# A fused attention and feed-forward kernel on one core: one program instead of two, the norm chain in items, eight probability slots and one split slot, with a new plan

## What is computed

```python
xn = layernorm(x)                                   # over the 256 features, eps 1e-5
q = einsum('bld,dhk->blhk', xn, Wq)                 # 16 heads of 64
latent = einsum('bld,dc->blc', xn, Wkv_down)        # 64 wide
k = einsum('blc,chk->blhk', latent, Wk_up)
v = einsum('blc,chk->blhk', latent, Wv_up)
attn = softmax(causal(einsum('bqhd,bkhd->bhqk', q, k) / 8))
y = einsum('bhqk,bkhd->bqhd', attn, v)
out = x + einsum('bqhd,hdo->bqo', y, Wout) + tanh(xn @ weight @ aux1 @ aux2 + bias)
```

## Time and profile before

| | us |
|---|---|
| median of 3 executions | 2101.32 (2099.3 to 2105.44) |
| the profiled execution | 2102.5 |
| its span in the trace | 2100.8 |
| PE busy | 2008.7 (96%) |
| DVE busy | 1651.9 (79%) |
| POOL busy | 1352.5 (64%) |
| ACT busy | 1108.7 (53%) |

### The profile page before, as it was taken

The page is one execution under the profiler, slowest core; times in us unless marked ns, Lnnn a source line. Parts: engine busy times, 40 slices in busy tenths (PEclk is TensorE's granted clock), DMA queues, the critical chain, the costliest instruction groups (busy, mean ns, idle before and its releaser), DMA issues.

```text
span 2100.8 us, 35430 instructions
## 1 busy us (share of the span) xinstructions
PE 2008.7 (96%) x11192; PEld 1329.4 (63%) x11192; DVE 1651.9 (79%) x3875; ACT 1108.7 (53%) x2075; POOL 1352.5 (64%) x1163
## 2 busy tenths in 40 slices
PE   7999999989999899999999999999999999999996
PEld 6666666656666566666666666666666666666563
DVE  4778778788778888778878878788878788778773
ACT  3455555545555455554555555555455555555553
POOL 0466666765666657676667756666567656667766
PEclk7999999999999999999999999999999999999998
DMA  3112111111111201121111211112111121111110
GB/s 99 32 34 60 37 41 42 37 54 35 47 37 42 59 24 42 47 62 37 45 34 37 67 37 37 39 40 62 37 37 37 44 59 37 42 37 34 52 36 25
DMA packets 83396, 91.37 MB, mean 43 GB/s; under 512 B 12304, under 2 KB 66448, under 8 KB 83216
## 3 DMA queue, kind: packets, MB, share of 16 engines
q1 hardware_dynamic: 83216, 89.11, 15.2%
HBM read 45.55 MB, written 8.91 MB: 26 GB/s over the span
## 4 chain that ended last, share of the span: by engine, by line
PE 71%; DVE 18%; issue 3%; DMA 2%; ACT 1%; SPq 1%; POOL 1%; POOLq 0%; ACTq 0%; DVEq 0%
PE ps L953 20%; PE ps L891 17%; PE ps L967 11%; PE ps L937 9%; PE ps L940 9%; DVE ps L1189 4%; PE ps L993 3%; DVE split_lo L1216 3%; DVE maxima L1194 2%; DVE rows L1205 1%; DVE xn L1281 1%; DVE y L1211 1%; DMA norm<-recips 1%; DVE stats L1251 1%; DVE maxima L1189 1%
## 5 line engine op out<-in xcount | busy, mean ns | idle before, releaser
L1335 POOL TENSOR_TENSOR p_sum<-p_sum,probs 128x512 f32<-128x512 f32 x672 | 899.8, 1366 | 264.1 <-ACT probs L1101 262.1
L1101 ACT ACTIVATE probs<-ps 128x512 f32<-128x512 f32 x1152 | 673.0, 597 | 461.3 <-PE ps L940 444.1
L1189 DVE CUSTOM_DVE_ANT_0 ps<-ps,causal 128x512 f32<-128x512 f32 (+3 forms) x1024 | 495.0, 502 | 160.3 <-PE ps L967 152.0
L953 PE MATMUL ps<-probs,latent 128*64 128x512 f32 x2304 | 525.7, 600 | 5.4 <-DVE q_lo L1305 5.4
L967 PE MATMUL ps<-k_hilo,q_hi 128*128 128x512 f32 (+3 forms) x1536 | 478.8, 362 | 22.4 <-DVE maxima L1189 14.1
L937 PE MATMUL ps<-q_hi,k_hilo 128*128 128x512 f32 x1152 | 479.6, 416 | 11.0 <-ACT probs L1101 9.9
L940 PE MATMUL ps<-q_lo,k_ones 65*128 65x512 f32 x1152 | 459.6, 399 | 0.0
L1335 POOL TENSOR_TENSOR p_sum<-probs 128x512 f32<-128x512 f32 x224 | 288.4, 1300 | 238.7 <-ACT probs L1101 237.5
L1194 DVE TENSOR_REDUCE maxima<-ps 128x1 f32<-128x512 f32 x512 | 352.0, 687 | 91.3 <-PE ps L967 88.1
L967 PEld LDWEIGHTS ps<-k_hilo,q_hi 128*128 128x128 f32 x1536 | 275.8, 191 | 130.4 <-issue 81.6
L953 PEld LDWEIGHTS ps<-probs,latent 128*64 128x64 f32 x2304 | 153.7, 137 | 306.8 <-issue 278.9
(11 more groups left out here) (101 smaller groups left out, 2326.1 us busy)
## 6 DMA issues: line engine op xcount, KB each, us to landing
q_hi<-q_hi SPq DMA_DIRECT2D x256, 128.0 KB, 2.4
norm<-recips SPq DMA_DIRECT2D x256, 128.0 KB, 2.9
x_in<-in_L_attn_x_bld SPq DMA_DIRECT2D x8, 1024.0 KB, 5.6
out_x<-acc SPq DMA_DIRECT2D x64, 128.0 KB, 1.7
q_lo<-rows SPq DMA_DIRECT2D x128, 4.0 KB
rows<-norm SPq DMA_DIRECT2D x128, 4.0 KB
recips<-rows SPq DMA_DIRECT2D x128, 4.0 KB
probs<-in_L_attn_Wq SPq DMA_DIRECT2D x1, 1024.0 KB, 7.7
```

The source lines that it names most:

```text
L953: last = nc.tensor.matmul(y_bank[g * LATENT:(g + 1) * LATENT, :], latent[par][:, key_block(unit, s), :], probs[:, t % PT_SLOTS, g * BANK:( ...
L1101: nc.scalar.activation(probs[:, t % PT_SLOTS, g * BANK:(g + 1) * BANK], ps[:, bank_of[kind, key], :], ACT.Exp).then_inc(exp_done, 1)
L1189: nc.vector.tensor_tensor_reduce(bank, bank, causal[:, BANK - w:BANK], 1.0, LOWEST, ALU.add, ALU.max, maxima[:, unit % 4, h, 0:1]).then_in ...
L1335: nc.gpsimd.tensor_tensor(sums, other, probs[:, slot, part], ALU.add).then_inc(pool_done, 1)
```

## The change

1. **One program.** `run` is called once with the two plans joined, so the barrier between them is gone, and engines pass from one plan to the other on their own. `bank_left` knows the last fold in a bank (kind `W`).
2. **First stage.** `x` of batch 0 comes by two DMAs with a semaphore each (later batches too), then Wq, Wk, and Wkv after those. `WARM` = 8 matmuls on the zeros of `causal` go ahead of the first transposes. The constants are made first on DVE, the fold of `wqk` stands around the second pair of transposes, `KN` after the queries, the remaining folds ahead of and between the eight maxima, and the subtractions for the low parts of `wvo` and `wff` after all maxima (`split wvo`).
3. **Repeated waits.** `wait_new` leaves out a wait of PE for a value that PE already waited for. On PE's matmuls 4,160 semaphores are named in place of 6,676.
4. **Norm chain in items.** LN1 is 13 items of one operation (the first: eight aggregations), planned 700 ns apart, each still followed by its own wait.
5. **Slots.** `SPLIT_SLOTS` 2 to 1, `PT_SLOTS` 7 to 8.
6. **The plan.** Other assumed costs and landings, extra time (`LATER`) before an item's input counts as ready, `SOON` 60 to 0, `LEAD` 13 to 11, feed-forward and the load of x earlier in a batch. PE goes 138 times to PVs and back instead of 133; the numbers of matmuls stay the same but for the 8 warm ones.

The diff, cut to its core:

```diff
-PT_SLOTS, Y_SLOTS, SPLIT_SLOTS, SUM_SLOTS, Q_BUFS = 7, 3, 2, 2, 3
+PT_SLOTS, Y_SLOTS, SPLIT_SLOTS, SUM_SLOTS, Q_BUFS = 8, 3, 1, 2, 3
-PE_TIME = {"ST": (462, 665), "PV": (846, 1070), "R": (462, 680), "MT": (60, 330), "O0": (693, 900),
+PE_TIME = {"ST": (462, 665), "PV": (859, 1080), "R": (462, 680), "MT": (60, 330), "O0": (715, 920),
...
-            "LN0": (800, 900), "LN1": (3000, 3200), "LN4": (1300, 1500)}
-LANDING = {"Q": 2900, "MT": 2300, "X": 6000, "RG": 2600, "RO": 2200, "RB": 4300}
+            "LN0": (800, 900), "LN1": (250, 350), "LN4": (1300, 1500)}
+LANDING = {"Q": 3500, "MT": 2300, "X": 7000, "RG": 3200, "RO": 2200, "RB": 4600}
+LATER = {"O": 2000, "R": 800, "MT": 800, "Q": 300}
-SOON = 60
-LEAD = 13
+SOON = 0
+LEAD = 11
-        self.f = [(b * STEPS + 3.5 * n + 1, (b, HALF_BLOCKS[n // 2][n % 2])) for b in range(batches)
+        self.f = [(b * STEPS + 3 * n + 1, (b, HALF_BLOCKS[n // 2][n % 2])) for b in range(batches)
-        self.x_at = [(b * STEPS + STEPS // 2 - 6, b + 1) for b in range(batches - 1)]
+        self.x_at = [(b * STEPS + STEPS // 2 - 12, b + 1) for b in range(batches - 1)]
...
                 if key[1] == 3:
-                    self.after(end, "LN1", key[0])
+                    for n in range(LN1_PARTS):
+                        self.after(end + 700 * n, "LN1", (key[0], n))
...
-                out.append((max(self.normal[u], bank), at, self.place_o))
+                out.append((max(self.normal[u] + LATER["O"], bank), at, self.place_o))
...
-            if late and (not st or step - late[1] > 1.5 or not idle_act):
+            if late and (not st or step - late[1] > 1.0 or not idle_act):
...
+    plan = [("W", "warm"), ("W", "constants")]
+    plan += [("LN0", (0, k)) for k in range(4)] + [("LN1", (0, n)) for n in range(LN1_PARTS)]
+    plan += [("LN4", (0, k)) for k in range(2)] + [("W", "turn wq"), ("W", "turn wk")]
+    plan += [("T", (0, c, 0)) for c in range(2)] + [("LN4", (0, k)) for k in range(2, 4)]
+    plan += [("TL", (0, c, 0)) for c in range(2)] + [("W", "casts"), ("W", "fold wqk 0")]
+    plan += [("T", (0, c, 1)) for c in range(2)] + [("TL", (0, c, 1)) for c in range(2)]
+    plan += [("W", "fold wqk 1")]
+    for side in range(2):
+        plan += [*two_parts("K", (0, side)), ("KL", (0, side))]
+    plan += [*two_parts("Q", (0, 0)), ("QL", (0, 0)), *two_parts("Q", (0, 1)), ("KN", 0)]
...
+            if what == "warm":
+                pe.wait_ge(consts_made, 1)
+                for n in range(WARM):
+                    nc.tensor.matmul(ps[:, 0, 0:BANK - P], causal[:, 0:P], causal[:, 0:BANK - P],
+                                     start=True, stop=True)
...
+            def wait_new(signal, value):
+                if reached.get(signal.num, 0) < value:
+                    reached[signal.num] = value
+                    pe.wait_ge(signal, value)
...
-        run(*first_plan(), load_all, make_constants)
-        run(*body_plan(B))
+        first, first_banks = first_plan()
+        body, body_banks = body_plan(B)
+        run(first + body, {**first_banks, **body_banks}, load_all, make_constants)
```

More of the change, by code:

```diff
@@ L195, in flush @@
                 if key[1] == 3:
-                    self.after(end, "LN1", key[0])
+                    for n in range(LN1_PARTS):
+                        self.after(end + 700 * n, "LN1", (key[0], n))
             elif kind == "LN1":
                 end = self.run("DVE", when, DVE_TIME[kind])
-                for k in range(2):
-                    self.after(end + 1000 * k, "LN4", (key, k))
+                if key[1] == LN1_PARTS - 1:
+                    for k in range(2):
+                        self.after(end + 1000 * k, "LN4", (key[0], k))
             elif kind == "LN4":
@@ L233, in choices @@
                 if q is not None:
-                    out.append((max(q, self.earliest("MAX")), self.max_at[self.n_max], self.place_max))
+                    out.append((max(q + LATER["Q"], self.earliest("MAX")), self.max_at[self.n_max], self.place_max))
         if "P1" in self.open:
@@ L239, in choices @@
             if self.turns:
-                out.append((max(self.max_end[self.turns[0]], bank), now - 9, self.place_mt))
+                out.append((max(self.max_end[self.turns[0]] + LATER["MT"], bank), now - 9, self.place_mt))
             if self.outs and self.block_added(self.outs[0][1]):
                 at, u = self.outs[0]
-                out.append((max(self.normal[u], bank), at, self.place_o))
+                out.append((max(self.normal[u] + LATER["O"], bank), at, self.place_o))
             if self.n_f < len(self.f) and (self.n_f < 2 or self.f[self.n_f - 2][1] in self.added):
@@ L292, in place_st @@
         if g == 1 and s == block_of(u):
-            self.sums.append((self.masked[-1], u))
+            self.sums.append((self.masked[-1] + LATER["R"], u))
     def place_max(self, ready):
@@ L489, in first_plan @@
 def first_plan():
[L492 to L502 removed]
+    plan = [("W", "warm"), ("W", "constants")]
[8 more added lines that the diff above has]
+    plan += [*two_parts("Q", (0, 0)), ("QL", (0, 0)), *two_parts("Q", (0, 1)), ("KN", 0)]
     maxima = [("MAX", c) for u in range(AHEAD) for c in max_chunks(u)]
[L504 to L506 removed]
+    plan += [("W", "turn others"), ("W", "fold aux"), *maxima[:2], ("QL", (0, 1)), maxima[2]]
+    plan += [("W", "fold wvo"), *maxima[3:6], ("W", "fold wff"), *maxima[6:]]
+    plan += [("MT", 0), ("W", "split wvo")]
     bank, n_p0, n_max = {}, 0, 0
@@ L515, in first_plan @@
         elif kind == "MT":
-            bank[kind, key] = 7
+            bank[kind, key] = 4
     return plan, bank
@@ L625, in build @@
         w_split = sem("w_split")
-        x_loaded = sem("x_loaded")
+        x_loaded = [sem(f"x_loaded{i}") for i in range(2)]
         ln_chain = sem("ln_chain")
@@ L864, in fold_on_dve @@
                         op1=ALU.subtract).then_inc(w_split, 1)
-            elif what == "fold wvo":
-                for n, bank in enumerate((5, 7, 6)):
-                    dve.wait_ge(w_copied, 14 + n)
+            elif what == "split wvo":
+                dve.wait_ge(w_copied, 17)
+                nc.vector.tensor_tensor(wff_lo[:, :, :].rearrange("p c n -> p (c n)"), ps[:, 0, :],
+                                        wff_hi[:, :, :].rearrange("p c n -> p (c n)").bitcast(F32),
+                                        ALU.subtract).then_inc(w_split, 1)
+                dve.wait_ge(w_copied, 18)
+                for n, bank in ((3, 1), (0, 5), (1, 7), (2, 6)):
                     nc.vector.tensor_tensor(wvo_part(wvo_lo, n), ps[:, bank, :],
@@ L1019, in tensor_program @@
                     b, c, half = key
-                    pe.wait_ge(xn_ready, 4 * count.of("LN1", b) + 2 * half + 2)
+                    wait_new(xn_ready, 4 * b + 2 * half + 2)
                     for k in range(4):
@@ new lines, in vector_program @@
+                    last = bits[:, 1, :].bitcast(F32) if n < 7 else guess
+                    if n == 0:
+                        for i in range(BLOCKS):
+                            done = nc.vector.bn_aggr(mean_var[:, i, :], stats[:, i, :])
+                    elif n == 1:
+                        done = nc.vector.tensor_scalar(var, mean_var[:, :, 1], EPS, None, ALU.add)
+                    elif n == 2:
+                        done = nc.vector.tensor_scalar(bits[:, 0, :], var.bitcast(I32), 1, None,
+                                                       ALU.logical_shift_right)
+                    elif n == 3:
+                        done = nc.vector.tensor_scalar(bits[:, 1, :], bits[:, 0, :], -1.0,
+                                                       RSQRT_BITS, ALU.mult, ALU.add)
+                    elif n % 3 == 1:
+                        done = nc.vector.tensor_tensor(square, last, last, ALU.mult)
+                    elif n % 3 == 2:
+                        done = nc.vector.scalar_tensor_tensor(
@@ L1274, in vector_program @@
+                    chained(done)
                 elif kind == "LN4":
@@ L1382, in sync_program @@
                     sp.wait_ge(ff_added, BLOCKS * key)
-                    sp.dma_start(x_in[:, :, :], x[key].rearrange("(i p) d -> p i d", p=P)
-                                 ).then_inc(x_loaded, 16)
+                    for half in range(2):
+                        sp.dma_start(x_in[:, 4 * half:4 * half + 4, :], x_rows(key, half)
+                                     ).then_inc(x_loaded[half], 16)
             for i in range(Q_BUFS):
```

176 lines of the change are left out of this document (75 added, 101 removed).

## The result

The changed kernel takes **2037.35 us** (median of 4, 2031.39 to 2040.17) against 2100.31 us (median of 4, 2099.17 to 2105.44). The ratio is 0.9694, with a 95% interval of 0.9675 to 0.9712. The forecast was 2053 us, in a range of 2022 to 2092. The profiled execution took 2039.62 us, its span 2037.7.

What follows compares the result with a forecast made beforehand. PE's work, 96% busy, plus what keeps PE from it, was taken as the bound. The sum 2102.5 - 22 - 12 + 0 + 1 - 16 = 2053.5 became 2053 us by the runs' median, range 2022 to 2092.

Steps and rivals of the forecast that it cites:

- Norm chain in items, -22: At six batch edges: less queueing on DVE, with x loaded earlier, saves 22 us, two thirds of 33.7.
- a maximum now waits for one or two of them: On DVE at batch edges: a maximum queues behind one or two chain operations, not the rest of the chain; part of -22.
- The upper end, 33.7 us: Most that six batch edges could give: 21.2 us of PE idle time above the usual plus 12.5 us of lower clock.
- DVE becomes the bound at batch edges: Rival: DVE, 87% busy at the edges and slowed by the lock with POOL, loses the 22 us; 2075 us, chance 0.18.
- First stage, -12: Start of the kernel up to the body's first matmul, in one program: 12 us less, bounds -5 and -17.
- Repeated waits, 0: PE's 2,516 fewer named semaphores gain nothing; bounds 0 and -8 us, at 3 ns each.
- Slots and turns, +1: Five more PE turns to PVs cost 1 us; the eighth slot itself shortens no row.
- The rival in which HI holds up ACT: Rival: with one split slot HI waits in ACT's queue, PE stands behind exponentials; 2131 us, chance 0.04.
- The end, 0: Last output matmuls still wait 9.97 us for the last unit's sums, reciprocals and split; no gain.
- The new plan, -16: PE idle between edges and DVE waits for spread reciprocals shrink with the new order: 16 us less, bounds -35 and +15.
- I take half of the lower end's size: Sizing of the new plan: -16 us taken from the -35 bound, which was all PE idle time between edges.
- and those remain: First stage's clock: the 32-matmul halves of L773, behind which the level was low, remain, so only 3 of 10.2 us were given.

Runs made afterwards that it cites:

- e2: Changed kernel with the 13 norm-chain items of each batch put together on DVE where the middle one stood, PE's order the same: 2013.85 us, ratio 0.9588.
- e6: Changed kernel with the 13 norm-chain items put together on DVE where the last of them stood: 2055.43 us, ratio 0.9796.
- e5: Changed kernel with the 13 norm-chain items put together on DVE where the first of them stood: 2058.6 us, ratio 0.9806.
- e1: Changed kernel with the old plan, old slots and norm chain in one piece; one program, new first stage and left-out waits kept: 2086.19 us, ratio 0.9929.
- e12: Kernel before, two programs and old order, with only PE's repeated waits left out: 2094.23 us, ratio 0.9972.
- e3: Changed kernel with 7 probability slots instead of 8, still 1 split slot, order the same: 2040.17 us, ratio 0.9714.
- e8: Changed kernel with 7 probability slots and 2 split slots, order the same: 2041.76 us, ratio 0.9728.
- e11: Kernel with the norm items grouped at the middle place, planned with earlier assumed landings, LATER at 0 and SOON at 60: 2099.6 us, ratio 0.9993.
- e9: Kernel with the norm items grouped at the middle place, with every repeated wait of PE written out again: 2017.75 us, ratio 0.9613.

## Why the prediction was right, and where not

The total came out 16 us below the forecast and in its range, but by terms that were off in both directions: about 16 us too much at the edges against some 25 too little for the plan, and some 8 for waits and end. That these nearly cancel is luck. Of the signs named, the chain's operations of up to 1.2 us with maxima between them, the body's start near 49 us and the shorter wait for the reciprocals came; PE's idle time at the edges under 12 us and the clock at 1.00 in most of them did not, and between the edges 11.4 us are idle, not 25.

- **Norm chain in items, -22: wrong.** The edges' idle time fell by 24.6 - 16.3 = 8.3 us, and the lower clock cost (29.24 - 25.09) / 2 = 2.1 more: -6, items and new plan together. The step that failed is "a maximum now waits for one or two of them". The plan put items 700 ns apart, but on DVE two low parts of queries (1.39 us) and the items themselves at up to 1.24 us ate the distance, and three ended up in a row. The upper end, 33.7 us, was real: e2 has no idle time and no lower clock left at the edges, by putting the chain together in the right place. The cut itself is neither good nor bad: 22 us worse than e2, 21 and 24 better than e6 and e5.
- **The rival "DVE becomes the bound at batch edges": wrong as put, right in its price.** e2 has DVE at 96% there and PE at 100%. But the duration of an item does rise from 0.17 to up to 1.24 us, as the rival priced it, and this is what makes the stalls. The rule of the Trainium skill behind it, page "SBUF — State Buffer", section "Who interferes with whom", is the lock on the port pair shared by DVE and GpSimd; that blocked operations end with POOL's addition agrees. The same section says that a tensor reduction never contends: the trace agrees, since the changed kernel's maximum (L1211) at 400.49 takes 0.69 us beside an addition, and all 512 of that line lie between 676 and 694 ns. So the lock hits the items and spares the maxima; I had applied it to a sum over items and not asked which of them would stand in a row.
- **First stage, -12: right.** e1 gives -14.9 with the waits, and e12 -5.9 for the waits alone: -9, with some 4 us of uncertainty. The transposes took 1.94 us against 3.55. The body's first score matmul stands at 48.12 us (forecast: near 49), but that is one draw out of a wide range (see below).
- **Repeated waits, 0: too small.** 5 to 6 us, within the stated end of 8. The stated bound of "3 ns each, less than the rows' last digit tells" was nearer than the value that I took.
- **Slots and turns, +1: right** within what e3 and e8 can tell. The rival in which HI holds up ACT fell: its wait for `y` went from 51.9 to 27.4 us.
- **The end, 0:** the last wait is 6.69 us where it was 9.97, so -3.
- **The new plan, -16: the sum's largest miss.** From e1 to e2 it is 72 us, of which the edges hold 25.0 idle and 18.18 / 2 = 9.1 of the 18.18 us of PE work that e1 had at the lower clock behind its edges: 34. So the plan gives about -38 elsewhere, or -35 without the end. What is left of the change itself, 64 - 6 - 9 - 5 - 3, is 41. Two steps failed. "I take half of the lower end's size": the idle time between edges fell from 34.0 to 11.4, by 22.6 us, two thirds of it. And the lower end counted idle time only, though the same paragraph says that short delays hide in PE's busy time; that is where the other 12 to 18 us have to be. The traces bear this out: without the 7.71 us of warm matmuls PE's busy time fell by 27.9 us, of which (23.8 - 11.8) / 2 = 6.0 are the first stage's clock and 1.6 its transposes, with the same matmuls. The reason given, that the waits were of inputs that came late, points the right way and further than it was followed: the wait for the reciprocals fell from 98.7 to 19.3 us and PE's for the split's low part from 24 times to 2, and without the later landings, `LATER` and `SOON` at 0 (e11) all of the time is lost. That it is these waits that bring it back in e11 is not shown.

**The first stage's clock.** In the ten traces that have this first stage with its warm matmuls, PE runs the same 237 matmuls up to MT, and the body's first score matmul stands anywhere from 45.17 us (e1) to 54.34 (e3); the old first stage has the body's first matmul at 60.95 in the kernel before and at 54.02 in e12. What differs is the clock. PE in e1, and in e3 (stretch, us, busy, PEclk):

```profile
8.00:46.30 38.30, 32.26 (x232) 1.00 0.31 83
```

```profile
10.00:16.80 6.80, 6.18 (x60) 0.99 1.07 310
16.80:30.40 13.60, 13.60 (x55) 0.50 0.00 0
```

So the 12.8 us by which the changed kernel's trace is ahead are in part the clock of two executions, and the -9 rests on the medians of e1 and e12. In the changed kernel's trace the folds of `wqk` (3.39 us each), the keys and the queries all ran at the full level; the step "and those remain" failed there, and held in e3. The lower level came later, for 13.6 us with 11.80 us of PE work, where the first program had it for 23.8 (the 20.4 us counted, and 3.4 from 45.1). What should follow by the Trainium skill, "TensorE: Matmul & The Clock Gate", section "What's actually happening", is the whole stage at the full level. That came in e1 and in none of the others; of the 7 us that I had put on it, e1's body starts 3.0 us earlier than the changed kernel's, and 9.2 earlier than e3's. In e3 the clock fell at 16.8, after a stretch in which PE was busy for 6.18 of 6.80 us; why there and not in e1 stays open.

The term at the edges and the one between them are each read from one trace of each kernel. Which of landings, `LATER` and `SOON` carries the plan, and whether part of e11's loss is at its edges, stays open. The items on the old plan alone were not tried either.

## What to carry to other kernels

When a planner assumes when inputs are ready, err on the late side: the three margins together were worth up to 85 us here. Before cutting a chain of tiny VectorE operations because it blocks the queue, look at what GpSimd and TensorE do beside it, and move the whole chain into a stretch where GpSimd pauses or runs short instructions (0.17 us an operation against 1.2) and TensorE has work that needs nothing of VectorE; here that is one `if` and 22 us. Cutting it is no sure gain: the whole chain took 2014 to 2059 us by its place, the cut one 2037 and 2055. Do not read a gain of a few us off the first stage of a single trace; its clock alone moved the body's start by 9 us. When bounding what a better order can give, don't stop at the idle time: some busy time is delay too.

## What was not expected of the hardware

- The same 20 DVE operations at the third batch edge add up to 4.0, 5.8, 7.3 or 8.0 us by their place beside POOL; beside a mask of 0.61 us an 8-element operation takes up to 0.64, beside an addition of 1.26 up to 1.24.
- A single wait of PE of 2.71 us was followed by 6.8 us at 1.2 GHz (412.2 to 419.0) in which PE was busy for 6.49 us. With every such wait gone (e2) the clock held 2.4 GHz through all six edges. So by the trace a short wait is paid nearly twice: 16.3 us of idle time and 29.24 / 2 = 14.6 of clock at the six edges, though e2 is only 22 us faster.
- With the same PE instructions in the same order, the first stage ran at 2.4 GHz from 8 us to the body's start in e1, and at 1.2 GHz for 20.4 us in e3 (16.8 to 30.4 and 37.2 to 44.0).
- A wait on a semaphore value that PE has already passed costs about 2 ns; 2,516 of them are some 5 us (e9 against e2), with an uncertainty of the same size; e12, the kernel before without its repeated waits, is 6 us faster, clear of noise.
